# End of a batch in a Perceiver block: norms turned one batch later, statistics placed behind the normalisation

## The reference

```python
x = x + cross_attention(layernorm(x), ctx_768, mask, Wq, Wk, Wv, Wo, bo)   # 8 heads of 64, 2048 keys
x = x + attention(layernorm(x), Wq2, Wkv2, Wo2)      # 16 heads of 64, over the axis of 8 batches x 128
x = x + ffn(layernorm(x), w_gate, w_up, w_down)      # activations rounded to 8 bits, weights to -1, 0, 1
```

## Time and profile before

| | |
|---|---|
| median of 3 runs | 767.38 us (766.2 to 770.09) |
| profiled execution, its own time | 768.35 us |
| its span, first to last instruction | 765.2 us (3.15 us of the time lie around it) |
| mean granted TensorE clock | 0.945 |
| busy share: PE, DVE, ACT, POOL | 87%, 58%, 47%, 14% |

### The profile page before, as it was taken

The page is one execution under the profiler, slowest core; times in us unless marked ns, Lnnn a source line. Parts: engine busy times, 40 slices in busy tenths (PEclk is TensorE's granted clock), DMA queues, the critical chain, the costliest instruction groups (busy, mean ns, idle before and its releaser), DMA issues.

```text
span 765.2 us, 14274 instructions
## 1 busy us (share of the span) xinstructions
PE 666.9 (87%) x4217; PEld 524.4 (69%) x4244; DVE 443.9 (58%) x960; ACT 356.4 (47%) x846; POOL 109.0 (14%) x143
## 2 busy tenths in 40 slices
PE   2898698979889779979879889999999899889996
PEld 1677587868778668868758667777777778534553
DVE  6823444554545453545567756666666544699974
ACT  2234233434434333434410146666666443568984
POOL 2681000010100110010100012222221100012121
PEclk9999798979989897989989989999999999999999
DMA  8000000000000000004169834445553343000111
GB/s 314 26 23 24 24 2 21 22 22 22 2 21 22 22 2 21 22 22 140 69 205 301 290 110 166 166 166 165 166 165 139 136 140 124 1 1 15 27 27 41
DMA packets 40067, 64.91 MB, mean 85 GB/s; under 512 B 4056, under 2 KB 20440, under 8 KB 40032
## 3 DMA queue, kind: packets, MB, share of 16 engines
q1 hardware_dynamic: 40032, 64.45, 25.1%
HBM read 53.95 MB, written 10.49 MB: 84 GB/s over the span
## 4 chain that ended last, share of the span: by engine, by line
PE 66%; DVE 13%; issue 9%; DMA 4%; ACT 3%; DVEq 3%; POOL 1%; SPq 1%; ACTq 0%; POOLq 0%
PE bank L587 35%; PE bank L717 6%; PE bank L949 5%; PE bank L705 3%; DMA absw<-in_L_ffn_w_down_dram 3%; PE bank L690 3%; PE bank L957 2%; PE bank L864 2%; DVE asum L1607 2%; DVE tern L1657 2%; PE bank L606 2%; DVE xn_a L1374 1%; PE bank L841 1%; PE bank L899 1%; PE bank L852 1%
## 5 line engine op out<-in xcount | busy, mean ns | idle before, releaser
L1069 ACT ACTIVATE probs<-probs,negm 128x256 f32<-128x256 f32 x104 | 52.1, 501 | 87.1 <-DVE negm L1472 86.5
L1472 DVE CUSTOM_DVE_ANT_0 probs<-bank,bias,negm_old 128x256 f32<-128x256 f32 x104 | 46.0, 480 | 42.4 <-PE bank L690 42.4
L949 PE MATMUL bank<-w_T,xqT 128*128 128x512 bf16 x248 | 57.3, 379 | 5.3 <-ACT xqT L1252 2.0
L717 PEld LDWEIGHTS bank<-v_sb,pT 128*128 128x128 f32 x416 | 52.3, 191 | 5.5
L484 POOL TENSOR_TENSOR rstd<-var_eps,neg_half 128x1 f32 (+1 forms) x16 | 10.0, 625 | 320.9 <-DVE var_eps L1535 249.8
L1363 DVE TENSOR_TENSOR kT_lo<-bank,kT_hi 128x512 fp32r<-128x512 f32 x28 | 19.4, 692 | 62.0 <-ACT kT_hi L1058 62.0
L717 PE MATMUL bank<-v_sb,pT 128*128 128x64 f32 x416 | 54.7, 274 | 0.0
L1062 ACT COPY v_sb<-bank 128x512 f32<-128x512 f32 x28 | 15.1, 590 | 76.5 <-PE bank L717 73.5
L690 PE MATMUL bank<-kT_hi,qT_hi 64*128 64x256 f32 x104 | 23.0, 433 | 29.6 <-issue 27.2
L949 PEld LDWEIGHTS bank<-w_T,xqT 128*128 128x128 bf16 x256 | 24.1, 98 | 34.9 <-issue 2.9
L587 PE MATMUL bank<-cxT_hi,wk_hi 128*128 128x256 f32 x168 | 38.4, 342 | 4.6 <-ACT cxT_hi L1052 4.6
(11 more groups left out here) (236 smaller groups left out, 1692.1 us busy)
## 6 DMA issues: line engine op xcount, KB each, us to landing
tern_dram<-tern SPq DMA_DIRECT2D x8, 768.0 KB, 5.4
tstage<-tern_dram SPq DMA_DIRECT2D x8, 768.0 KB, 4.4
cx<-in_ctx_dram SPq DMA_DIRECT2D x14, 384.0 KB, 3.0
absw<-in_L_ffn_w_gate_dram SPq DMA_DIRECT2D x8, 512.0 KB, 3.8
absw<-in_L_ffn_w_up_dram SPq DMA_DIRECT2D x8, 512.0 KB, 5.4
absw<-in_L_ffn_w_down_dram SPq DMA_DIRECT2D x8, 512.0 KB, 6.8
tern_raw<-in_L_ffn_w_gate_dram SPq DMA_DIRECT2D x8, 512.0 KB, 6.4
tern_raw<-in_L_ffn_w_up_dram SPq DMA_DIRECT2D x8, 512.0 KB, 7.1
```

Of the source, the lines that this page charges most:

```text
L717: last = mm(bank[7][:, h * DH:(h + 1) * DH], pT[:, g % 2, at:at + P], v_sb[:, t, h * DH:(h + 1) * DH], start=(t == 0), stop=(t == CT - 1))
L949: last = mm(bank[3 + 2 * which + c % 2][:], xqT[:, u, k * P:(k + 1) * P], w_T[:, which, k, c * 512:c * 512 + 512], start=(k == 0), stop=(k ...
L1069: fn(probs[:, h, :], probs[:, h, :], ACT.Exp, bias=negm[:, h:h + 1], scale=-1.0, accum_out=csum[:, h:h + 1]).then_inc(p_done, 1)
L1472: nc.vector.tensor_tensor_reduce(probs[:, h, :], bank[3 + h % 2][:, 0:CHUNK], bias[:], -SCALE, negm_old[:, h:h + 1], ALU.add, ALU.min, neg ...
```

## The change

Five things move, and no arithmetic is added or removed. On DVE the statistics go behind the normalisation and the next query's low part; the low part of a norm is made one batch later. On PE a norm is transposed one batch later, and first of its batch end. On POOL the residual waits for the norm. Of the last two norms the very last gets a buffer and a bank of its own (`on_c`, bank 5). The four `wv2_lo` go behind all norms, and the third terms of the second values of g = 0 and 1 go behind their first two.

```diff
@@ residual loop of POOL
             with pool.Fori(1, B - 1) as b:
                 rsqrt(b - 1, var_c, rstd_c)
+                pool.wait_ge(xn_c_done, START + b)
                 residual(b)
@@ PE, turn(g) in a chunk
                     if g == 1:
-                        pe.wait_ge(lnT_lo, START + b - 2)
+                        pe.wait_ge(lnT_lo, START + b - 3)
@@ PE, end of a batch
+            def turn_norm_last():
+                pe.wait_ge(xn_c_done, START + B)
+                pe.wait_ge(onT_lo, START + B)
+                for k in range(DK):
+                    last = tr(bank[5][:, k * P:(k + 1) * P], xn_last[:, k * P:(k + 1) * P], ident[:])
+                last.then_inc(lnT_ps, 1)
...
                 pe.wait_ge(negm_done, START + H * chunks)
+                with pe.If(b > 2):
+                    turn_norm(b - 3)
                 with pe.If(b > 0):
                     project_output(b - 1)
                 turn_output(b)
-                with pe.If(b > 1):
-                    turn_norm(b - 2)
+            turn_norm(B - 3)
             project_output(B - 1)
             turn_norm(B - 2)
-            turn_norm(B - 1)
+            turn_norm_last()
...
-            for g in range(G):
-                if g >= 2:
-                    pe.wait_ge(v2_act, START + g - 1)
-                    pe.wait_ge(v2_dve, START + g - 1)
+            for g in range(2):
+                second_values(g, 0, (0, 1))
+                second_values(g, 1, (0, 1))
+            for g in range(2):
+                second_values(g, 0, (2,))
+                second_values(g, 1, (2,))
+            for g in range(2, G):
+                pe.wait_ge(v2_act, START + g - 1)
+                pe.wait_ge(v2_dve, START + g - 1)
                 second_values(g, 0)
                 second_values(g, 1)
@@ ACT, end of a batch
+                with act.If(b > 2):
+                    norm_high(b - 3)
                 with act.If(b > 0):
                     projected(b - 1)
                 output_high(b)
-                with act.If(b > 1):
-                    norm_high(b - 2)
-
+
+            norm_high(B - 3)
@@ DVE, end of a batch
+                normalise(b, chunks)
+                with dve.If(b < B - 1):
+                    query_low(b + 1)
                 with dve.If(b > 1):
                     norm_stats(b - 2)
-                normalise(b, chunks)
+                with dve.If(b > 2):
+                    norm_low(b - 3)
                 with dve.If(b > 1):
                     norm(b - 2)
-                with dve.If(b < B - 1):
-                    query_low(b + 1)
                 output_low(b)
-                with dve.If(b > 1):
-                    norm_low(b - 2)
@@ DVE, behind the last batch
+            norm_low(B - 3)
             norm_stats(B - 2)
-            values_low(0)
             residual_last()
             norm_stats(B - 1, 1)
             norm(B - 2)
-            values_low(1)
-            norm(B - 1, 1)
+            norm_last()
             norm_low(B - 2)
-            values_low(2)
-            norm_low(B - 1)
-            values_low(3)
+            norm_low(B - 1, 5)
+            for k in range(DK):
+                values_low(k)
```

More of the change, by code:

```diff
@@ L133, in bass_perceiver_block_kernel @@
         on_c = at("on_c", 162, D)
+        xn_last = on_c
         o_all = at("o_all", 164, B, D)
@@ L805, in _, with second_values @@
-            pe.wait_ge(lnT_hi, START + B)
-            for g in range(G):
-                if g >= 2:
-                    pe.wait_ge(v2_act, START + g - 1)
-                    pe.wait_ge(v2_dve, START + g - 1)
+            turn_norm_last()
+            VALUE2_TERMS = (("hi", "hi"), ("lo", "hi"), ("hi", "lo"))
+            def second_values(g, half, terms=(0, 1, 2)):
+                for i in terms:
+                    a, c = VALUE2_TERMS[i]
+                    for k in range(DK):
+                        if g == 0 and half == 0:
+                            if a == "lo" and k == 0:
+                                pe.wait_ge(lnT_lo, START + B)
+                            elif c == "lo":
+                                pe.wait_ge(wv2_lo, START + k + 1)
+                            elif a == "hi":
+                                pe.wait_ge(wv2_hi, START + k + 1)
+                        last = mm(bank[2 * (g % 2) + half][:], part(ln_T, a)[:, k, g * P:(g + 1) * P],
+                                  part(wv2, c)[:, k, half * 512:half * 512 + 512],
+                                  start=(i == 0 and k == 0), stop=(i == 2 and k == DK - 1))
+                if 2 in terms:
+                    last.then_inc(v2_ps, 1)
@@ L1101, in output_high, with norm_high @@
                 cp(onT.hi[:].rearrange("p k q -> p (k q)"), bank[5][:]).then_inc(onT_hi, 1)
-            def norm_high(b):
+            def norm_high(b, of=6):
                 act.wait_ge(lnT_ps, START + b + 1)
@@ L1106, in norm_high @@
                 cp(to.rearrange("p k g a q -> p k (g a) q"),
-                   bank[6][:].rearrange("p (k g q) -> p k g q", k=DK, q=16)).then_inc(lnT_hi, 1)
+                   bank[of][:].rearrange("p (k g q) -> p k g q", k=DK, q=16)).then_inc(lnT_hi, 1)
             def projected(b):
@@ L1145, in _ @@
             norm_high(B - 2)
-            norm_high(B - 1)
+            norm_high(B - 1, 5)
             def weights_high(m):
@@ L1521, in output_low, with norm_low @@
                 low(onT.lo[:].rearrange("p k q -> p (k q)"), bank[5][:], onT.hi[:].rearrange("p k q -> p (k q)")).then_inc(onT_lo, 1)
-            def norm_low(b):
+            def norm_low(b, bank_of=6):
                 dve.wait_ge(lnT_hi, START + b + 1)
@@ L1526, in norm_low @@
                     "p k g a q -> p k (g a) q")
-                low(of(ln_T.lo), bank[6][:].rearrange("p (k g q) -> p k g q", k=DK, q=16), of(ln_T.hi)).then_inc(lnT_lo, 1)
+                low(of(ln_T.lo), bank[bank_of][:].rearrange("p (k g q) -> p k g q", k=DK, q=16), of(ln_T.hi)).then_inc(lnT_lo, 1)
             def norm_stats(b, slot=0):
@@ L1584, in residual_last, with norm_last @@
                 tt(x_all[:, B - 1, :], x_all[:, B - 1, :], bank[4][:], ALU.add).then_inc(x_mid, 1)
+            def norm_last():
+                dve.wait_ge(rstd_c, START + B)
+                dve.wait_ge(onT_ps, START + B)
+                ts(xn_last[:], x_all[:, B - 1, :], mv[:, 1, 0:1], rstd[:, B - 1:B], ALU.subtract, ALU.mult).then_inc(xn_c_done, 1)
+            norm_low(B - 3)
             norm_stats(B - 2)
-            values_low(0)
             residual_last()
```

## The result

The changed kernel takes a median of 762.4 us (22 runs, 758.56 to 768.96) beside 766.98 us of the kernel before (22 runs, 761.06 to 770.35): 0.995 of it, with a 95% interval of 0.9927 to 0.9973. Single runs of either kernel scatter by some 10 us, so the profile must say which terms of the sum this was. Ratios leave out runs over 1.5% above the fastest of their kernel: one of the six of e12 (758.77 is the median of all six), and two of the 19 of the kernel before that stand beside e5 and e8. The profiled execution of the changed kernel took 760.37 us, its span is 758.3, its mean granted clock 0.951.

The account below looks back on a forecast made before the run. The last wait of DVE's sequencer at each batch end was taken to set the next chunk. 768.35 - 4.6 - 0.3 + 0.5 = 763.95, on an execution 0.97 above the median, so 763.0 us; range 759.0 to 767.0.

Parts of the forecast that it names:

- What sets the next chunk: Batch ends: the next chunk starts when DVE's sequencer is through with the last wait, +6.00 before, then walks 3.79 us.
- Ends of batches 2 to 6: From `o_all` addition to next chunk: +9.1 us each; four ends save about 0.67, batch 5 saves 1.9, together -4.6.
- Ends of batches 0 and 1: These two ends lose some skipped branches; at most a few tenths, counted as -0.3 us.
- The collision with POOL: DVE operations held beside POOL's residual: priced at nothing where `qT_lo` is held; batch 5's 1.25 lies inside its 1.9.
- the price of 2.1: Skill page's reading: the blocked 1.07 of `qT_lo` and 1.05 of `xn_c` added up; not used in the sum.
- Behind the last batch: After the last addition: batch 5's transposes stand ahead of `project_output(7)`, so it and the transfers behind come 0.5 us later.
- POOL's wait: `residual` waits for `xn_c`; in the loop nobody waits for it, and it takes away a collision with DVE.
- Own buffer and bank, `wv2_lo` last, third terms later: Behind the loop: second values start some 1.5 us earlier, covered by a transfer; third group's wait grows to about 2; gain nothing.
- The clock: At the mean, 12 matmuls take 5.34 at the lower level, 2.67 at full; possible gain up to 2.7, left out of the sum.
- Rival B: Forecast sum plus the clock saving of 2.7 at the mean, from a longer wait before the third group: 760.3; chance 0.34.
- an earlier start is therefore passed on in full: Next chunk: everything starts from DVE's first score operation, so an earlier start there carries through the chunk undiminished.

Follow-up runs that it names:

- e12: Second set of runs of e2's kernel (norms only turned one batch later), beside the kernel before: median 758.77 us, ratio 0.9863.
- e5: Changed kernel without POOL's wait for the norm before the residual: median 764.15 us, 0.9975 of the kernel before.
- e8: Changed kernel with the loop's norm made on ScalarE in place of DVE, the shift by POOL: median 756.32 us, 0.9913 of the kernel before.
- e3: Kernel before with only DVE's order changed, statistics and `xn_c` behind normalisation and `qT_lo`, turn as before: median 779.69 us, ratio 1.0183.
- e9: Changed kernel with 14 semaphore raises on DVE's sequencer behind `onT_lo` in each batch end: 774.97 us, one run.
- e10: Changed kernel with 14 semaphore raises on PE's sequencer behind the output's transposes in each batch end: 755.48 us, one run.
- e2: Kernel before with only the turn of a norm and its low part one batch later, statistics still first, no POOL wait: median 758.47 us, ratio 0.9912.
- e4: Kernel before with eight matmuls, result never read, keeping PE busy ahead of the mean: median 766.09 us, ratio 0.9996.
- e6: Changed kernel as it is, since register additions meant for DVE's sequencer were dropped from the trace: 762.07 us, one run.
- e7: Changed kernel as it is, since register additions meant for PE's sequencer were dropped from the trace: 759.17 us, one run.

## Why the forecast held, point by point

**What sets the next chunk: right, and shown.** From the branch row behind the batch end to the chunk it is 3.71 before, 3.69 after, 3.69 in e5 and 3.70 in e3, with ends from 8.83 to 12.43; a delay of DVE's sequencer passes on about one for one (e9), a delay of PE only beyond about 1.9 (e10, batch 3). This is shown for batches 2 to 6, not for 0 and 1.

**Ends of batches 2 to 6: right, under-sized.** I counted -4.6 and the trace has -5.83 (four times 0.91 to 0.93, and 2.15). The statistics started at +2.51 where I had +2.72, because they follow `qT_lo` without a gap, and `xn_c` came at +5.03 for +5.23. What I had not seen is which of the two moves on DVE earns this: e3 shows that the statistics' move alone costs 1.05 to 2.7 an end, e2 that without it the turn alone reaches 8.64. The full change is its turn minus a bare `rstd`.

**Ends of batches 0 and 1:** -0.98 for -0.3. Across all kernels the first of them varies from 7.45 to 8.52 where the code is nearly the same, so I would not lean on it.

**The collision with POOL: right at nothing.** The trace shows it plainly (1.75 for 0.69 in e2), and four ends do not move. It costs where the held operation leads to the last wait: 0.24 in batch 5 of e2, part of the longer ends of e3, and about 1.25 in batch 5 of the kernel before, which is in the sum. The Trainium skill, "SBUF — State Buffer", section "SBUF: two separate sides", has VectorE and GpSimd lock the shared ports against each other, so that one of them fully blocks. These held operations agree that one holds the other up, but not to the full: `xn_c` in e5 started with 0.95 of POOL's row still to run and was longer by 0.68. And the price of 2.1, by adding up what was held, does not come: what is held has already been handed over by the sequencer that everybody waits for (162.00 in e5).

**Behind the last batch:** the load came 0.27 later, for 0.5, and the wait before the third group grew to 2.02, for about 2. POOL's wait, which I had priced for the loop alone, is worth 2.4 here (e5, one execution).

**Own buffer and bank, `wv2_lo` last, third terms later: at nothing, and nothing was found.** The second values start 2.15 earlier and wait it off.

**The clock.** Rival B's saving of 2.7 is in the profiled execution (3.27 for 5.95), but not for B's reason: the wait of 2.02 did not bring the lower level (1.17 for the four matmuls behind it), PE is not late, the loads were quicker. Since e4 removes that idleness and does not move the median, I put the saving down to the pair of executions that were profiled, not to the change; e4's interval does not exclude a part of it. Leaving it out of the sum was right; a chance of 0.34 for it was too much.

**What I had left out:** the profiled pair differs by 8.0 of its own time and the medians by 4.6. All ends together give -6.8, but the last addition came only 3.70 earlier: the first addition, ahead of which the code is the same, is 1.39 later, and the seven stretches from a chunk's first score operation to the next batch's addition add up to 225.74 in place of 224.04, longer or shorter by up to 1.6 each as the stretch at the lower clock falls. So the step "an earlier start is therefore passed on in full" did not hold. The later first addition is scatter: it is at 82.67 in e6 and 85.84 in e7, which ran the changed kernel as it is. Of the stretches, e6 and e7 have 226.28 and 224.86, and e4, whose loop is that of before, 222.37; five traces suggest that the change gives back some 2 us there, and no more than that. The rest of the 8.0 lies behind the last addition: 1.99 up to the mean, 2.68 from there to `kT` and 1.06 outside the span, with 1.45 lost behind `kT`. That the median met the forecast to 0.6 is thus partly two errors that cancel: an under-sized gain, and a part given back in the chunks that I had only allowed for in the range.

## What to carry to other kernels

Where a stage begins with a loop that an engine's sequencer must walk, look for the last wait ahead of it, not for the busiest engine: a round trip over two other engines costs its full length there, while work already handed over is free even when it is held to more than twice its time. Price each move of a change by itself: here the turn earned everything, and the statistics' new place cost by itself 14 us. And before a wait at a join is called a property of the kernel, see it in several executions: PE's wait for the mean lay anywhere from none (e10) to 2.57.

## What the runs showed that I had not expected

- From one raised semaphore to the next DVE's sequencer takes 0.09 us and PE's 0.15; the latter's branch rows in the same walk take 0.21, DVE's 0.06. An empty window costs DVE's sequencer about 0.8 us, so three of them are most of the 3.7 in which it computes nothing.
- The one run with PE delayed (e10) took 755.48, less than all 22 of the changed kernel, although its seven ends add up to 5.0 more than those of the changed kernel. Its seven stretches between the ends take 219.8 in place of 225.7, and this goes with the clock: 27.9 us of them are at the lower level, in place of 41.6. Over all 14 traces the stretch behind a given batch is longer by 0.44 to 0.47 us for each us of it at the lower level; the one behind batch 0, for example, takes 17.91 at a mean granted clock of 0.91 in e10 and 19.95 at 0.81 in the changed kernel. The stretches at the lower clock begin earlier in e10 against the chunk's start (at 117.3, 3.8 before the chunk behind batch 1; in the changed kernel at 120.1, 0.4 behind it), so that part of them falls on PE's idle walk. The other gains of this execution lie behind the loop (1.7 up to the mean, 2.6 behind `kT`). That the delay of PE is what moved the lower stretches is one execution's word and is left open.
- ScalarE's norm (scale and shift from two 128x1 operands) takes 0.81, DVE's 0.55, and is the cheaper one here.
